# Twelve-stage decoder, last routed stage: eight tiles of y instead of four, listed slots in a loop of their own by two, the output stored tile by tile, and routed stages that end without emptying GpSimd's queue

## What is computed

```python
x = x + _L3_xattn_ref(_layernorm(x, axis=-1), ctx_1024, ...)
x = x + _L3_ffn_ref(_layernorm(x, axis=-1), L3_ffn_gate_weight, L3_ffn_gate_up_proj, L3_ffn_down_proj)
return x
```

```python
router_probs = softmax(x @ gate_weight.T)
top_v, top_i = jax.lax.top_k(router_probs, 4)
top_v = top_v / jnp.clip(top_v.sum(axis=-1, keepdims=True), 1e-12)
for each expert (w1, w2, we):          # w1: 192 x 256, w2: 256 x 96
    gate, up = jnp.split(x @ w1.T, 2, axis=-1)
    acc = acc + (silu(gate) * up @ w2.T) * we[:, None]
```

## Time and profile before

| | us |
|---|---|
| median of 3 runs | 1649.76 (1648.12 to 1654.68) |
| the profiled execution, its own time | 1653.33 |
| its span, first to last instruction | 1651.5 |
| last routed stage and output (from L145 of that stage) | 1450.1 to 1651.5 |

### The profile page before, as it was taken

How to read it: one execution, slowest core, us unless ns; L and a number is a source line. 1 busy time by engine, 2 the same in 40 slices (tenths; PEclk the granted TensorE clock), 3 DMA queues, 4 the chain that set the end, 5 groups by cost and what they waited for, 6 DMA issues and landing times. The chain is left out here.

```text
span 1651.5 us, 21016 instructions
## 1 busy us (share of the span) xinstructions
PE 1092.3 (66%) x5890; PEld 697.9 (42%) x5890; DVE 1084.3 (66%) x1811; ACT 486.0 (29%) x947; POOL 601.7 (36%) x608
## 2 busy tenths in 40 slices
PE   7445547998228785556998205798929788748950
PEld 3211135775015661114555204575714334447840
DVE  6999975864676549997985893310446778563452
ACT  3323312333402343331210102233203256603320
POOL 0046614553763115660000470134341532116645
PEclk9769977999559897997999557798969789969985
DMA  5064257995312305427000011504420230098843
GB/s 185 30 254 152 102 168 221 313 315 186 103 43 61 95 3 178 152 77 245 1 1 1 5 17 29 167 17 136 137 64 0 70 86 4 3 252 256 234 125 100
DMA packets 134866, 189.49 MB, mean 115 GB/s; under 512 B 34592, under 2 KB 97715, under 8 KB 133373
## 3 DMA queue, kind: packets, MB, share of 16 engines
q1 hardware_dynamic: 100300, 139.10, 26.8%
q0 software_dynamic: 12800, 29.55, 6.3%
q10 hardware_dynamic: 21680, 19.80, 3.8%
HBM read 143.59 MB, written 31.92 MB: 106 GB/s over the span
## 5 line engine op out<-in xcount | busy, mean ns | idle before, releaser
L165 POOL TENSOR_SCALAR rstd<-moments 128x4 f32<-128x4 f32 x24 | 6.5, 269 | 405.1 <-DVE moments L148 405.1
L177 PE MATMUL psum<-w_ident,h 128*128 128x128 f32 x144 | 29.4, 385 | 112.3 <-DVE h L155 112.3
L558 PE MATMUL psum<-l1s_read,w_ident 128*128 128x512 f32 x128 | 65.2, 635 | 52.5 <-DVE l1s_read L623 52.5
L558 PE MATMUL psum<-l0s_read,w_ident 128*128 128x512 f32 x128 | 65.6, 638 | 51.7 <-DVE l0s_read L623 51.7
L1841 DVE TENSOR_REDUCE l3x_neg<-psum 128x2 f32<-128x512 f32 x128 | 80.6, 683 | 24.3 <-PE psum L1712 24.3
L546 POOL TENSOR_TENSOR l1s_drive<-l1s_du,l1s_bc 128x1024 f32<-128x1024 f32 x32 | 75.3, 2353 | 35.3 <-DVE psum L619 35.3
L546 POOL TENSOR_TENSOR l0s_drive<-l0s_du,l0s_bc 128x1024 f32<-128x1024 f32 x32 | 75.2, 2352 | 35.3 <-DVE psum L619 35.3
L1816 ACT ACTIVATE l3x_work<-psum 128x512 f32<-128x512 f32 x128 | 72.7, 599 | 51.3 <-PE psum L1735 51.0
L1038 POOL DMA_INDIRECT l3f_x<-l3f_h_rows,l3f_token_of x64 | 59.3, 927 | 59.2 <-DVE l3f_token_of L1383 28.6
L1156 PE MATMUL psum<-l0f_w_in,l0f_xT 128*128 (+1 forms) x224 | 77.2, 468 | 0.1
L1029 POOL DMA_INDIRECT l0f_x<-l0f_h_rows,l0f_token_now x56 | 58.3, 1041 | 47.3 <-PE psum L1146 17.9
(11 more groups left out here) (632 smaller groups left out, 3154.5 us busy)
## 6 DMA issues: line engine op xcount, KB each, us to landing
l0f_w_in<-in_l0f_w_in SPq DMA_DIRECT2D x56, 352.0 KB
l0s_bc<-l0s_scratch SPq DMA_DIRECT2D x16, 1024.0 KB, 5.1
l1s_bc<-l1s_scratch SPq DMA_DIRECT2D x16, 1024.0 KB, 5.1
l3f_w_in<-in_l3f_w_in SPq DMA_DIRECT2D x32, 384.0 KB
l0f_w_down<-in_l0f_w_down SPq DMA_DIRECT2D x56, 176.0 KB
l2f_w_in<-in_l2f_w_in SPq DMA_DIRECT2D x24, 352.0 KB
l0f_y_rows<-l0f_y ACTq DMA_DIRECT2D x56, 128.0 KB
l3f_y_rows<-l3f_y ACTq DMA_DIRECT2D x68, 96.0 KB
```

The source lines that it names most:

```text
L177: ins = nc.tensor.transpose(m.psum[:, at:at + P], m.h[:, t, k * P:(k + 1) * P], m.ident[:])
L558: ins = nc.tensor.matmul(m.pair(2 + c)[:, cols], lhsT=m.ident[:], rhs=rhs[:, cols], start=start, stop=stop, skip_group_check=True)
```

## The change

1. `y` of the last routed stage has ROWS = 8 tiles and eight semaphores `y_stored`, so the copy of slot d waits for the store of slot d-8.
2. Listed slots leave the pipeline. They run after it in a loop with LISTED = 2 slots a turn, with their own tiles (`listed_x`, `listed_y`), own places for weights (32 and 33 of a store of now 34) and own semaphores. A turn does each operation for both slots and then the next. The least number of slots is then 66, and with 65 needed it is also the number that runs: one turn. The gathers and weight loads of the listed slots no longer wait for the places of own slots.
3. The output is stored by SP in the last stage itself, a tile of 128 KB as soon as its four additions are done. The blocks `clear11` and `store` go.
4. The block of all three routed stages is made with `no_gpsimd_drain=True`.
5. The ring of tiles for the gathers back is 24 long in all stages, on semaphores that the three stages share and never clear. The unused rows of `y_rows` are filled in 20 DMAs of half the size (stage 5, before 10).

```diff
-    y = ring("y", [P, D], GROUP)
+    y = ring("y", [P, D], ROWS)
+    listed_x, listed_y = (ring(s, [P, D], TURN) if narrow else None for s in ("listed_x", "listed_y"))
...
-    with nc.Block(name=tag + "block") as block:
+    with nc.Block(name=tag + "block", no_gpsimd_drain=True) as block:
...
-            def listed(base, s):
+            def fetch_listed(base, s):
                 e = sp.value_load(owners[0:1, bass.ds(base + s, 1)], min_val=0, max_val=E - 1)
...
+                sp.wait_ge(listed_down, base + (s + 1 - E))
+                sp.sem_inc(may_load, 1)
+                for w, name in ((w_in, "w_in"), (w_down, "w_down")):
+                    sp.dma_start(w[:, AHEAD + s, :, :].rearrange("p c x -> p (c x)"), source(name, e)).then_inc(listed_w_loaded[s], 16)
...
+            if out is not None:
+                for t in range(TILES):
+                    sp.wait_ge(accumulated, (t + 1) * K)
+                    sp.dma_start(out[:, t, :], m.resid[:, t, :]).then_inc(out_stored, 16)
+                sp.wait_ge(out_stored, 16 * TILES)
...
+            def turn_listed(base):
+                for s in range(TURN):
+                    pe.wait_ge(listed_x_loaded[s], base * (16 // TURN) + (16 - E // TURN * 16))
+                    turn_lanes(listed_x[s], s).then_inc(listed_x_turned, 1)
+                for s in range(TURN):
+                    pe.wait_ge(listed_xT, base + (s + 1 - E))
+                    pe.wait_ge(listed_w_loaded[s], base * (32 // TURN) + (32 - E // TURN * 32))
+                    in_lanes(s, AHEAD + s).then_inc(listed_in, 1)
+                for s in range(TURN):
+                    pe.wait_ge(listed_gate, base + (s + 1 - E))
+                    pe.wait_ge(listed_y_ready, base + (s + 1 - E))
+                    down_lanes(s, AHEAD + s).then_inc(listed_down, 1)
...
             if narrow:
-                own_then_listed(pe, E, groups, step_lanes, 2)
+                pe.sem_inc(listed_x_turned, TURN)
+                pe.sem_inc(listed_down, TURN)
+                for s in range(E + 2):
+                    step_own(s)
+                pe.wait_ge(xT_ready, E)
+                pe.wait_ge(y_ready, E + 1)
+                with pe.Fori(E // TURN, groups) as i:
+                    turn_listed(i * TURN)
...
-                    if not first or d >= GROUP:
-                        dve.wait_ge(y_stored[d % GROUP], base * (16 // GROUP) + (d // GROUP + 1) * 16)
-                    nc.vector.tensor_copy(y[d % GROUP][0:L, :], y_ps[d % 2][0:L, :]).then_inc(y_ready, 1)
+                    if d >= ROWS:
+                        dve.wait_ge(y_stored[d % ROWS], d // ROWS * 16)
+                    nc.vector.tensor_copy(y[d % ROWS][0:L, :], y_ps[d % 2][0:L, :]).then_inc(y_ready, 1)
...
-        with nc.Block(name="store") as block:
-            @block.sync
-            def _(sp):
-                for group in m.w_loaded:
-                    m.wait_weights(sp, group)
-                sp.dma_start(out, m.resid[:]).then_inc(stored, 16)
-                sp.wait_ge(stored, 16)
```

More of the change, by code:

```diff
@@ L746, in experts @@
     PAD = 8 - top
-    BLOCKS, GROUPS, RUNNING, FEWEST = block_counts(E, K, ahead, L)
+    BLOCKS, GROUPS, TURN, FEWEST = block_counts(E, K, ahead, L)
+    RUNNING = max(E, ahead)
     AHEAD = ahead
     narrow = E > ahead
-    assert BLOCKS <= P and (not narrow or chunks == 1 and E % GROUP == 0 and FEWEST == E // GROUP + 1)
+    assert BLOCKS <= P and (not narrow or chunks == 1 and E % TURN == 0 and FEWEST == E // TURN + 1)
     GONE, NONE = -3e38, -2e38
@@ L796, in experts @@
     up = ring("up", [P, F], 2) if shared else None
-    ROWS, backs = (len(sems) for sems in m.gather_sems[tag])
+    x_loaded, back_loaded, back_before = m.gather_sems[tag]
+    ROWS = len(x_loaded)
     x = ring("x", [P, D], ROWS)
     xT = ring("xT", [P, KD, P], 2)
-    w_in = sb(tag + "w_in", [P, ahead, KD, 2 * F])
-    w_down = sb(tag + "w_down", [rows, ahead, chunks, D])
+    w_in = sb(tag + "w_in", [P, ahead + (TURN if narrow else 0), KD, 2 * F])
+    w_down = sb(tag + "w_down", [rows, ahead + (TURN if narrow else 0), chunks, D])
     place = lambda base, s: base + s & (ahead - 1)
@@ L987, in _ @@
                 groups = group_count(sp)
-                with sp.Fori(RUNNING // GROUP, groups) as i:
-                    for s in range(GROUP):
-                        listed(i * GROUP, s)
+                with sp.Fori(E // TURN, groups) as i:
+                    for s in range(TURN):
+                        fetch_listed(i * TURN, s)
             else:
@@ L1214, in _, with turn_lanes, in_lanes @@
-            if narrow:
-                own_then_listed(pe, E, groups, step_lanes, 2)
+            def turn_lanes(src, i):
+                for k in range(KD):
+                    ins = nc.tensor.transpose(xT_ps[i][:, k, 0:L], src[0:L, k * P:(k + 1) * P], m.ident[0:L, 0:L])
+                return ins
+            def in_lanes(i, at):
+                for f in range(2):
+                    for k in range(KD):
+                        ins = nc.tensor.matmul(feature_ps[i][:, f, :], lhsT=w_in[:, at, k, f * F:(f + 1) * F], rhs=xT[i][:, k, 0:L],
+                                               start=(k == 0), stop=(k == KD - 1))
+                return ins
@@ L1282, in _ @@
             if narrow:
-                own_then_listed(act, E, groups, step_lanes, 3)
+                for s in range(E + 3):
+                    step_own(s)
+                with act.Fori(E // TURN, groups) as i:
+                    take_listed(i * TURN)
             else:
@@ L1437, in _ @@
+            if narrow:
+                dve.sem_inc(listed_y_ready, TURN)
+                for s in range(E + 2):
+                    step_own(s)
+                with dve.Fori(E // TURN, groups) as i:
+                    gate_listed(i * TURN)
             elif weights is None:
@@ L1474, in _ @@
                 nc.vector.scalar_tensor_tensor(
[L1475 removed]
+                    out=m.resid[:, t, :], in0=back[q % BACKS], scalar=weight[:, c, t:t + 1], in1=m.resid[:, t, :],
                     op0=ALU.mult, op1=ALU.add).then_inc(accumulated, 1)
@@ L2773, in decoder @@
             lambda n, j: softmax_attention(m, n, j, "l3x_", heads=32, causal=False),
-            lambda n, j: experts(m, n, j, "l3f_", rows=96, chunks=1, normalize=True, floor=1e-12),
+            lambda n, j: experts(m, n, j, "l3f_", rows=96, chunks=1, normalize=True, floor=1e-12, out=out),
         ]
```

226 lines of the change are left out of this document (120 added, 106 removed).

## The result

The changed kernel takes 1638.53 us in the median of 5 runs (1636.94 to 1640.71), the kernel before 1650.03 in 5. The ratio is 0.9927, with a 95% interval of 0.9908 to 0.9945: 12.0 us faster (9.1 to 15.2). Forecast were 1628.5 us and a range of 1622.5 to 1637.0. The time lies 1.5 us above the range. The profiled execution took 1640.07 us.

The account below looks back on a forecast made before the run. No engine's sum bounds the kernel; waits for stores of y set the last routed stage's first half. Gains 8.2 + 4.0 + 7.7 + 1.4 = 21.3 us take the median from 1649.76 to 1628.5 us, range 1622.5 to 1637.

Parts of the forecast that it names:

- The two other routed stages: Ahead of stages 3 and 9: no longer emptying POOL's queue shortens the gaps, gain 1.4 us (0 to 1.5).
- The end: Program's end: no emptying of POOL's queue or extra blocks, last tile stored right behind DVE's last addition; gain 7.7 us.
- Emptying the queue isn't removed but shows elsewhere: Rival, chance 0.08: the next stage's first POOL work and the program's end wait for it; gain 17.4, 1632.4 us.
- Eight tiles: Last routed stage's own slots: 11.3 us lost to the four-tile ring of y; eight tiles gain 8.2 us (5.1 to 11.3).
- the stores never stop DVE: Rival, chance 0.22: with eight tiles no store of y holds DVE up in the last routed stage; gain 24.4, 1625.4 us.
- The bound on weights: Last routed stage: weights may lag, their last pair ending near 1557 while PE needs it near 1572.
- The wait moves: Rival, chance 0.06: PE, let go, is stopped as long by x or weights; first term 0, gain 13.1, 1636.7 us.
- Listed slots: Last own slot to first gather back: one turn outside the pipeline takes T + 10.5 instead of T + 14.5; gain 4.0 us.
- The gathers back: Last routed stage: their issue at 1.28 us each sets this part, not the ring; 24 tiles for 20 change nothing.
- slower: Case, chance 0.02: PE runs own slots at the lower clock, 1.28 us more each; all 64 would give 1710 us.

Follow-up runs that it names:

- drain_back: The changed kernel with l0f and l2f again ending by emptying GpSimd's queue, only the last routed stage without; 1627.14 us, ratio 0.9826 to the kernel before.
- before_without: The kernel before, with l0f and l2f ending without emptying GpSimd's queue; 1661.88 us, ratio 1.0038 to the kernel before.
- empty_twice: The changed kernel, with GpSimd's queue emptied once more in l0f and l2f between gathers of x and gathers back; 1633.28 us, ratio 0.9861.
- drain_back_again: The changed kernel with the default end in l0f and l2f, rerun on one chip beside the changed kernel; 1628.9 us, ratio 0.9860 to the kernel before.

## Why the prediction was wrong

**The step that failed** is "The two other routed stages": "Emptying POOL's queue is the difference: 0.5 + 1.0", a gain of "**1.4 us** (0 to 1.5)". It took what stuck out of the cover in the earlier trace rows for the whole price. Shown (drain_back, before_without, empty_twice): the price is 8.6 and 3.0 us, it isn't removed but passed to the next block that ends by default, and 8.0 and 2.3 us of it had been hidden by DVE's additions. The term is -10.3 instead of +1.4. That is 11.7 us, more than the whole miss. The size stood in the prediction itself: "The end" found 7.9 us between POOL's last gather and the stage's end, and put them down to the same work in the last stage.

The rival *Emptying the queue isn't removed but shows elsewhere* named the mechanism, but priced it at the last end alone and gave "the next stage's first work of POOL" nothing. The blocks `clear{n}` stand between, and meet with every engine.

**Eight tiles** (8.2, from 5.1 to 11.3): the ring was the limit, as said, and 8.6 us came in the profiled execution. That 8.2 came so near is partly luck. It stood for a stall of which a part stays, and no part stayed: in none of the eleven kernels with eight tiles does DVE wait for a store of `y`, which is the rival *the stores never stop DVE*. Over all kernels four tiles take 89.3, 91.1 and 93.6 us for 61 slots, and eight take 78.7 to 81.7: 10.9 us between the means.

What kept the changed kernel at 80.66 us instead of 78.0 lies in four slots. PE had waited 5.2 us for the first gathered `x`, until 1497.3. The first two slots, from 1501.4 to 1505.2, then took 2.45 and 1.40 us. The granted clock was 0.50 until 1502 (the 1.2 GHz level) and 0.65 in the mean of the next 3 us. In the kernel before the first slot took 1.67 us, so some of the 11.3 us "lost" was never the ring's. Two later ones took 1.62 and 2.21, the second behind a wait of 0.7 us for `w_down`. PE, changed kernel, columns as in the earlier trace rows:

```profile
1500.00:1502.00 2.00, 2.00 (x12) 1.86 (x12) 0.35 (x2) 0.82 (x3) 1.61 (x2) 0.50 0.36 94
1502.00:1505.00 3.00, 3.00 (x22) 2.67 (x21) 1.22 (x4) 0.82 (x3) 2.17 (x3) 0.65 0.23 68
```

The bound on weights held: no wait of PE for them above 0.7 us. But a little of the rival *The wait moves* is there. In seven of the eleven kernels PE waits behind slot 0 for gathered `x`, 0.5 to 2.4 us in all, as in drain_back_again from 1493 to 1585:

```profile
PE psum L1186 <- DMA l3f_x<-l3f_h_rows,l3f_token_of: 2.1, 3, 1.1
```

**Listed slots** (4.0): 3.8 in the profiled execution. Five kernels with the pipeline need 14.5 to 16.6 us, nine with the loop 10.3 to 11.8: 4.4 between the means. The forecast chain of T + 10.5 came out at 10.76 in the profiled execution.

**The gathers back** (0): -0.2 us.

**The end** (7.7): 8.7. The last 128 KB were over after 2.4 us instead of 3.0, and the span before ended at 1651.5, 0.4 us later than the prediction's 1651.1. Its 1645.8 for the end of the stage before is short as well: the emptying was over at 1646.2.

**The clock**: 1.00 was granted in the stretch from 1508 to 1556. Among the changed kernel's own slots only the first two show the lower level, and the case *slower* did not come near.

By terms: 8.6 + 3.8 - 0.2 + 8.7 = 20.9 where 19.9 were forecast, 1.3 in the stage's beginning and 1.3 in the rest of the program, which nothing forecast and which is within what executions differ by, and -10.3: 13.2 us, against 1653.33 - 1640.07 = 13.3. With that part undone the kernel takes 1627.1 and 1628.9 us, close to the forecast 1628.5, but the fit flatters the other terms. They add up to 19.9 us. Against the kernel before on the same chip these runs are 28.8 us (25.2 to 32.5) and 23.1 us (19.7 to 26.6) faster: the second interval takes 19.9 in, the first doesn't. The first run's chip had the slower kernel before (1656.0 us). What made its gain larger than the terms stays open.

## What to carry to other kernels

A fence (a point where an engine must have finished, or emptied, what it was given) has a price that isn't the gap it leaves: subtract nothing until you have found where its record ends, what else ended then, and which fence comes next and inherits the work. Ask of each wait that you remove whether it does work that somebody must do, and if it does, leave it where it is covered or move it to where its engine is idle. Here the covered end of the stage, the end of the next stage and the middle of GpSimd's list in addition were not told apart: their ratios to the kernel before are 0.983, 0.984 and 0.986, with intervals that overlap. A ring that is too short behind a busy DMA can be worth its full stall: the weights here had some 15 us of slack by the prediction's estimate, and no store of `y` held DVE up any more.

## What the runs showed of the hardware

- Emptying GpSimd's queue costs 0.082 us for each indirect DMA issued since the last time (1.36 us for 16 to 8.56 for 104, at a block's end), with all output landed too (8.06 for 98). With none since the last emptying it took 0.04 to 0.05 us. ACT's DRAIN in the same block took 8 to 14 ns.
- The time can be paid in instalments: emptied after 56 and again after 48, it cost 4.9 and 4.0 us. After 20 and again after 16, it cost 3.5 and 1.4, where 1.7 was expected of the first; that difference stays open.
- Queues don't hold a fixed share of busy DMA engines: with eight tiles ACT's went from 21.5% to 28.1% of the engines' time, SP's from 62.1% to 53.0%, and the total from 309 to 329 GB/s.
